# Recurrent layer with experts on one core: position network started earlier, part of VectorE's additions moved to GpSimd, all orders new

## The chip, the cores and the metric

One core of a Trainium2 chip runs the whole program. The metric is the device time of one execution in microseconds (us). The trace is one profiled execution of the same program. PE is TensorE, DVE is VectorE, ACT is ScalarE, POOL is GpSimd, SP is the engine that issues most transfers.

## The reference, cut to what matters

```python
xn = layernorm(x)                                  # x: 8 x 512 x 128, float32
u, v = split(silu(xn @ uv_w))                      # both 8 x 512 x 128
t = rpe(positions) * 0.99 ** |position|            # 3 layers of 32, then an output layer
s = (u * circular_convolution(t, v)) @ o_w         # through a transform of length 1024
rw = softmax(xn.mean(axis=1) @ Wr + br)            # one routing for each of the 8 batches
e1, e2 = top2(rw)                                  # two of 8 experts, weights by softmax
h = gelu(xn @ W1[e] + b1[e])                       # 128 -> 512, for both experts
y = sum_e weight_e * (h @ W2[e] + b2[e]) + xn
g = silu(layernorm(y) * gamma + beta)
out = x + s * g
```

`rpe` is a small network (width 32): three times `h = silu(ln(h)) @ fc`, then an output layer, on the positions 0 to 511 and their negatives.

## The kernel before

Every engine has its own instruction stream, written by hand in Python. What stands in a stream, and in which order, is set by tables (`PE_JOBS`, `ACT_JOBS`, `DVE_JOBS`, `POOL_JOBS`): each names a kind of job and, for each repetition, a place. The places are counted in tiles. A tile is one slice of 128 hidden units of one expert of one batch: 8 tiles a batch (2 experts of 4 slices), 64 in all. For tile n PE computes the hidden slice (`hidden`, bank0 or bank1; from tile 4 on in three matmuls of the types fp32r, L1119 to L1121, over an upper and a lower part of both operands), ACT applies Gelu into `h_ring` (L624), and PE multiplies by W2 (`expert_out`, L1332). Between the tiles stand the other jobs. On each engine the order is strict: a job that waits holds all that stands behind it. Place 10.03 means after the work of tile 10; places under 0 are the head.

The jobs that the text speaks of:

- `mean`, `logits`, `rank`, `shift`, `hot`, `top`, `mix`, `pick`, `sel`, `bias`: the router, for batch 0, batch 1 and batches 2 to 7 together. `rank` gives the indices with which SP fetches W1 (`w1_raw`) and W2 (`w2_s`) of the batch.
- `x_stats` (DVE), `x_root` (POOL), then normalising: `x_norm` on DVE (L772) for batches 0 and 1, `x_affine` on ACT (L490) for the rest; `x` is the transpose on PE, `x_out` the copy on ACT, `x_hi` and `x_lo` split it.
- `weights` (DVE), `rows` (PE), `matrices` (DVE), then `product`, `square`, `variance`, `eps`, `layer`, `root`, `spread`, `norm`, `tanh`, `act`: the position network.
- `w1_hi` makes the upper part of W1, `w1` on DVE the lower one (L818, 128 x 512).
- `forth` is the transform of v (six matmuls), `products`, `middle` and `join` its products with the filter on DVE, `back` the transform back (L1367), `odd` and `conv` its reading and the product with u, `mixed` the multiplication by o_w (L1391).
- `out` on DVE reads the expert sum of a batch (L808, L810), `y` transposes it (L1376), `sum` is its statistics, `root` on POOL its inverse root, `y_affine` on ACT, `norm` on DVE multiplies by gamma and adds beta (L1044, L1046), `gate` is the tanh or Silu, `weight` and `result` finish the gate and the output (L1094 multiplies, L1097 adds x).
- `lift` and `settle` do this for batch 7, with POOL giving only the root.
- `warm` is matmuls of zeros, `WARM[i]` of them in job i. `warm(0)` is also called once before the tables. Each of these matmuls leaves two records in the trace.

## Time and profile before

| | |
|---|---|
| median of 3 runs | 213.66 us (211.11 to 214.86) |
| profiled execution, time | 214.19 us |
| profiled execution, span from first to last instruction | 212.4 us |
| outside the span | 1.8 us |
| PE, DVE, ACT, POOL busy | 199.2, 171.3, 122.8, 47.0 us |
| mean granted clock of PE | 0.967 |

PE's busy time counts pipelined matmuls from issue to a modelled end, so a full PE in this table need not be at its peak rate. Work is judged by the distance from one start to the next.

### The profile page before, as it was taken

What the parts mean: (1) busy time and instruction counts of PE and PEld (TensorE: products, weight loads), DVE (VectorE), ACT (ScalarE), POOL (GpSimd) and SP (SyncE); (2) the same over time, 40 slices, a digit from 0 to 9 for tenths busy, and PEclk for the clock granted to TensorE, in tenths of its full rate; (3) what the DMA queues carried; (4) which work ended last, traced back from release to release, by engine and by line L of the source; (5) the groups of instructions that cost most, each with busy time, mean ns of one, the idle gap of its engine ahead of it and who ended that gap; (6) DMA issues with size and microseconds to landing.
All of it is one profiled execution on the core that took longest, in us unless ns stands there. A gap on an engine that the chain in (4) does not pass through costs nothing.

```text
span 212.4 us, 3224 instructions
## 1 busy us (share of the span) xinstructions
PE 199.2 (94%) x926; PEld 140.6 (66%) x926; DVE 171.3 (81%) x451; ACT 122.8 (58%) x269; POOL 47.0 (22%) x72
## 2 busy tenths in 40 slices
...
DMA packets 25173, 17.37 MB, mean 82 GB/s; under 512 B 1396, under 2 KB 22556, under 8 KB 25028
## 3 DMA queue, kind: packets, MB, share of 16 engines
...
q8 instruction: 7, 0.11, 0.2%
...
## 4 chain that ended last, share of the span: by engine, by line
PE 49%; DVE 21%; POOL 12%; issue 11%; ACT 4%; DMA 1%; DVEq 0%; POOLq 0%; ACTq 0%
PE bank L1332 13%; PE bank L1119 6%; PE bank L1120 5%; PE bank L1121 5%; PE bank L1367 4%; PE bank L1231 3%; PE bank L1172 3%; POOL rstd L678 3%; POOL layer_r L698 2%; DVE Y L991 2%; DVE ystats L745 2%; DVE prod L993 2%; POOL root L676 2%; DMA x_ring<-in_L_attn_x 1%; POOL mr L714 1%
## 5 line engine op out<-in xcount | busy, mean ns | idle before, releaser
L1332 PE MATMUL bank<-h_ring,w_s 128*128 128x512 f32 x128 | 66.4, 602 | 1.5 <-issue 0.8
L624 ACT ACTIVATE h_ring<-bank,b_sel 128x512 f32<-128x512 f32 x64 | 43.8, 688 | 37.4 <-PE bank L1121 32.9
L1119 PE MATMUL bank<-xT_hi,w_hi 128*128 128x512 f32 x60 | 41.5, 691 | 0.7 <-ACT h_ring L624 0.7
L676 POOL TENSOR_SCALAR root<-ymv 128x4 f32<-128x4 f32 x7 | 4.2, 606 | 111.6 <-DVE ymv L748 111.6
L1332 PEld LDWEIGHTS bank<-h_ring,w_s 128*128 128x128 f32 x128 | 23.3, 189 | 8.2 <-issue 2.2
L1120 PE MATMUL bank<-xT_lo,w_hi 128*128 128x512 f32 x60 | 23.7, 394 | 0.0
L1121 PE MATMUL bank<-xT_hi,w_lo 128*128 128x512 f32 x60 | 23.6, 393 | 0.0
L1119 PEld LDWEIGHTS bank<-xT_hi,w_hi 128*128 128x128 f32 x60 | 11.3, 189 | 11.5 <-issue 9.8
L1120 PEld LDWEIGHTS bank<-xT_lo,w_hi 128*128 128x128 f32 x60 | 11.4, 190 | 9.9 <-issue 9.8
L1367 PEld LDWEIGHTS bank<-inv_sb,Y 128*128 128x128 f32 x128 | 15.3, 192 | 3.3 <-issue 2.9
L1367 PE MATMUL bank<-inv_sb,Y 128*128 128x128 f32 x128 | 15.7, 276 | 0.3 <-DVE conv L1028 0.2
L991 DVE TENSOR_TENSOR Y<-bank,A_sb 128x1024 f32<-128x1024 f32 x8 | 9.7, 1216 | 5.9 <-PE bank L1121 5.9
L500 ACT ACTIVATE zb<-bank,ynmr,yrstd 128x128 f32<-128x128 f32 x28 | 10.5, 458 | 5.6 <-POOL ynmr L691 5.5
L1116 PE MATMUL bank<-h_ring 128*128 128x256 f32 x40 | 12.4, 468 | 1.4 <-DVE h_ring L961 1.4
L1121 PEld LDWEIGHTS bank<-xT_hi,w_lo 128*128 128x128 f32 x60 | 11.3, 188 | 2.6
L554 ACT ACTIVATE w_s<-w_s,cw_all 128x512 f32<-128x512 f32 x16 | 10.9, 718 | 0.3 <-DMA w_s<-in_L_ffn_W 0.3
L1116 PEld LDWEIGHTS bank<-h_ring 128*128 128x128 f32 x40 | 9.1, 239 | 2.9 <-DVE h_ring L961 1.4
L1391 PE MATMUL bank<-ow_sb,uT 128*128 128x128 f32 x64 | 8.5, 276 | 2.7 <-DVE uT L1030 2.7
L1391 PEld LDWEIGHTS bank<-ow_sb,uT 128*128 128x128 f32 x64 | 8.0, 192 | 4.3 <-DVE uT L1030 3.1
L818 DVE TENSOR_TENSOR w_lo<-w_raw,w_hi 128x512 fp32r<-128x512 f32 x15 | 10.1, 682 | 0.8 <-ACT w_hi L547 0.7
L490 ACT ACTIVATE xn<-x_ring,mr,rstd 128x128 f32<-128x128 f32 x24 | 9.9, 489 | 0.1
L993 DVE TENSOR_TENSOR prod<-bank,A_sb 128x1024 f32<-128x1024 f32 x8 | 9.7, 1214 | 0.0
...
## 6 DMA issues: line engine op xcount, KB each, us to landing
...
```

The source lines that it names most:

```text
L500: last = nc.scalar.activation(zb[:, b % 2, t], YT_PS[:, t * D:(t + 1) * D], ACT.Identity, bias=ynmr[:, t:t + 1], scale=yrstd[:, t:t + 1])
L554: nc.scalar.activation(w2_s[:, b % 2, j].rearrange("p c d -> p (c d)"), w2_s[:, b % 2, j].rearrange("p c d -> p (c d)"), ACT.Copy, scale=c ...
L624: nc.scalar.activation(h_ring[:, n % NH], H_PS[n % 2][:], ACT.Gelu, bias=b1_sel[g][:, c, j, r:r + 1]).then_inc(h_done, 1)
L991: nc.vector.tensor_tensor(y, both(v_re), filters(kc, 1 - s, 1), ALU.mult).then_inc(vre_used, 1)
L993: nc.vector.tensor_tensor(term, both(v_im), filters(kc, 1 - s, 0), ALU.mult).then_inc(vim_used, 1)
L1116: nc.tensor.matmul(H_PS[1][:, 0:PW], h_ring[:, 0, 0:P], h_ring[:, 0, 0:PW], start=True, stop=True)
L1119: nc.tensor.matmul(out_ps, w_hi, m_hi, start=start, stop=False)
L1120: nc.tensor.matmul(out_ps, w_hi, m_lo, start=False, stop=False)
L1121: return nc.tensor.matmul(out_ps, w_lo, m_hi, start=False, stop=stop)
L1332: nc.tensor.matmul(OUT_PS[:], w2_s[:, b % 2, j, c], h_ring[:, n % NH], start=(i == 0), stop=(i == HT - 1)).then_inc(w2_mm, 1)
L1367: last = nc.tensor.matmul(EO_PS[:, o:o + P], Y[:, kc, s, ri, b % GB], inv_sb[:, kc, ri], start=(kc == 0), stop=(kc == KC - 1))
L1391: last = nc.tensor.matmul(S_PS[b][:, t * P:(t + 1) * P], uT[:, b, t * P:(t + 1) * P], ow_sb[:], start=True, stop=True)
```

## The change

Four things change together. The names of lines below are those of the kernel after.

1. Position network: `position_weights` is split into `start`, which comes before the first `rank`, and `weights` (the output layer's matrix), which comes late. Its small results lie in the last two rows of `uT` and in bank3, so the first product no longer needs the second one (`rows`). Product, variance, root and spread of layer 0 now stand in the head.
2. Normalising of batches 2 to 7 goes from ACT (`x_affine`) to DVE (`x_norm`).
3. POOL takes the lower parts of W1 from batch 3 on (10 of 15), the addition of beta for batches 0 to 5, and the last addition of x for batches 0 to 6. That is 23 instructions of 128 x 512. The factor 0.5 moves into DVE's multiplication.
4. `WARM` is `[5, 1, 1, 2]` with job 0 only in the explicit call, so 9 matmuls of zeros are left of 20. All tables are new; the first tile with `u` and `v` is 12 and was 10.

```diff
-WARM = [5, 5, 3, 2]
+WARM = [5, 1, 1, 2]
...
+    ("beta", 0): [12.04, 31.01, 34.01, 50.01, 55.01, 57.02],
+    ("w1", 6): [16.01, 17.01, 22.01, 22.02, 30.01, 30.02, 37.01, 37.02, 45.01, 46.01],
+    ("add", 0): [40.01, 42.01, 44.01, 57.01, 63.01, 63.02, 63.04]})
...
-        y0, y1 = rows[:, 0], rows[:, 1]
+        y0, y1 = uT[:, B - 2], uT[:, B - 1]
...
+                        if n < B - 1:
+                            sp.wait_ge(res_done, n + 1)
+                        else:
+                            sp.wait_ge(last_done, h + 1)
...
+            def w1_lower(i):
+
+                b, j = i // TOPK, i % TOPK
+                pool.wait_ge(w1_hi_done, i)
+                nc.gpsimd.tensor_tensor(w1_lo[:, b % 2, j], w1_raw[:, j], w1_hi[:, b % 2, j],
+                                        ALU.subtract).then_inc(w1_split, 1)
+
+            def gate_beta(b):
+
+                pool.wait_ge(zm_done, b + 1)
+                nc.gpsimd.tensor_tensor(zb[:, b % 2], zb[:, b % 2], bcast(bet[:].unsqueeze(1), [P, NT, D]),
+                                        ALU.add).then_inc(zg_done, 1)
+
+            def add_x(b):
+
+                pool.wait_ge(s_read, b + 1)
+                pool.wait_ge(x_in[b], 32)
+                nc.gpsimd.tensor_tensor(x_ring[:, b], th_ring[b % NTH], x_ring[:, b], ALU.add).then_inc(res_done, 1)
...
-            def position_weights(_):
+            def position_start(_):
 
                 dve.wait_ge(rpe_in, 16 * 8)
                 dve.wait_ge(consts_in, 16)
...
                 if n == 0:
-                    pe.wait_ge(rpe_ready, 2)
+                    pe.wait_ge(rpe_ready, 1)
+                    pe.wait_ge(xmean_done, 1)
...
+                if b < PLAIN:
+                    gained.then_inc(zm_done, 1)
+                    return
+                step(gained)
+                dve.wait_ge(zg_done, b)
...
+                dve.wait_ge(s_ps, b + 1)
+                if b < B - 1:
+                    nc.vector.scalar_tensor_tensor(out=w, in0=S_PS[b][:].rearrange("p (t d) -> p t d", t=NT),
+                                                   scalar=0.5 if b < PLAIN else 1.0, in1=w, op0=ALU.mult,
+                                                   op1=ALU.mult).then_inc(s_read, 1)
+                    return
```

PE from its first instruction to its second hidden slice. `bank1<-h_ring` are the zeros, `rstd,x_ring` is `mean`, `x_ring,w1_raw` a hidden slice. Before:

```order
L1116 MATMUL bank1<-h_ring 128x256 x5
L1127 MATMUL bank5<-wr_sb,h_ring 128x8
L1116 MATMUL bank1<-h_ring 128x256 x10
L1136 MATMUL bank4<-rstd,x_ring 128x1 x4
...
L1116 MATMUL bank1<-h_ring 128x256 x3
L1259 MATMUL bank5<-c128,onehot0 8x1 x2
L1116 MATMUL bank1<-h_ring 128x256 x2
L1271 MATMUL bank5<-selT0,conv 128x2 x4
L1295 MATMUL bank4<-c128,rows 128x8
L1296 MATMUL bank4<-rows,yT 128x224
L1136 MATMUL bank2<-rstd,x_ring 128x1 x4
L1311 MATMUL bank0<-x_ring,w1_raw 128x512
```

After:

```order
L1150 MATMUL bank1<-h_ring 128x256
L1170 MATMUL bank4<-rstd,x_ring 128x1 x4
...
L1215 MATMUL bank4<-yT,uT 128x256
L1150 MATMUL bank1<-h_ring 128x256
L1296 MATMUL bank5<-c128,onehot0 8x1 x2
L1226 MATMUL bank4<-same_mean,rows 128x4 x2
L1182 MATMUL bank6<-c128,xn 128x128 x4
L1308 MATMUL bank5<-selT0,conv 128x2 x4
L1150 MATMUL bank1<-h_ring 128x256 x2
L1347 MATMUL bank0<-x_ring,w1_raw 128x512
```

One matmul of zeros instead of ten stands between the router's constants and `mean`, and the mean of batch 1 and the `rows` went behind the first hidden slice.

DVE from the expert sum of batch 7 (`yT<-bank2`) to its end. Before:

```order
L808 SCALAR_TENSOR_TENSOR yT<-bank2,b2_mix2,x_ring 128x2x128
L810 SCALAR_TENSOR_TENSOR yT<-bank2,b2_mix2,x_ring 128x2x128
L1027 TENSOR_TENSOR conv<-bank3,O_sb 128x2x128
...
L1094 TENSOR_TENSOR cs_raw<-bank6,cs_raw 128x512
L1097 SCALAR_TENSOR_TENSOR x_ring<-cs_raw,x_ring 128x512
L1056 SCALAR_TENSOR_TENSOR zb<-bank5,ymv,gam 128x128 x4
L1027 TENSOR_TENSOR conv<-bank3,O_sb 128x2x128
L1028 TENSOR_TENSOR conv<-bank3,O_sb 128x2x128
L1030 TENSOR_TENSOR uT<-uT,conv 128x512
L1066 SCALAR_TENSOR_TENSOR zb<-zb,yrstd,bet 128x128 x4
L1094 TENSOR_TENSOR th<-bank7,th 128x512
```

After:

```order
L836 SCALAR_TENSOR_TENSOR yT<-bank2,b2_mix2,x_ring 128x2x128
L1121 SCALAR_TENSOR_TENSOR cs_raw<-bank4,cs_raw 128x512
L1121 SCALAR_TENSOR_TENSOR cs_raw<-bank6,cs_raw 128x512
L771 BN_STATS ystats<-bank5 128x6 x4
L774 BN_AGGR ymv<-ystats 128x2 x4
L1121 SCALAR_TENSOR_TENSOR th<-bank7,th 128x512
L1092 SCALAR_TENSOR_TENSOR zb<-bank5,ymv,gam 128x128 x4
L1102 SCALAR_TENSOR_TENSOR zb<-zb,yrstd,bet 128x128 x4
```

Both `conv` of batches 6 and 7 went ahead of this piece, and three multiplications of batches 4, 5 and 6 without their additions stand in it.

POOL at its end in the kernel after (before, only the groups of `root`, `ynmean`, `yrstd` and `ynmr` stood here):

```order
L685 TENSOR_TENSOR yrstd<-root,minus_half 128x4
L698 TENSOR_TENSOR ynmr<-ynmean,yrstd 128x4
L752 TENSOR_TENSOR x_ring<-cs_raw,x_ring 128x512 x2
L691 TENSOR_SCALAR root<-ymv 128x4
L692 TENSOR_TENSOR yrstd<-root,minus_half 128x4
L752 TENSOR_TENSOR x_ring<-th,x_ring 128x512
```

Two additions of x come ahead of the last root, one behind it.

## Rows read from the trace of the kernel before

**Rows 1.** The page's first line.
```profile
span 212.4 us, 3224 instructions
```
**Rows 2.** Windows: busy PE, PEld, DVE, ACT, POOL; clock; DMA.
```profile
34.05:147.54 113.49, 112.44 (x538) 81.06 (x538) 93.23 (x229) 81.80 (x186) 24.16 (x35) 1.00 0.25 72
147.54:164.96 17.42, 16.77 (x65) 10.99 (x64) 15.83 (x27) 9.35 (x17) 4.02 (x4) 1.00 0.42 122
164.96:180.18 15.22, 14.96 (x53) 9.16 (x51) 15.05 (x26) 8.22 (x13) 2.33 (x4) 1.00 0.18 52
180.18:197.72 17.54, 16.41 (x80) 11.12 (x80) 15.30 (x32) 10.09 (x19) 2.05 (x4) 1.00 0.11 31
197.72:212.40 14.68, 6.93 (x58) 6.33 (x56) 11.02 (x33) 1.63 (x5) 1.27 (x2) 0.87 0.30 89
```
**Rows 3.** The timeline of the head: start, us, engine, line.
```profile
5.59 1.02 POOL L708 TENSOR_TENSOR rstd<-var_eps,minus_half 128x4 f32<-128x4 f32 x1 [4.60 <-DVE neg_mean L759]
6.16 5.14 PE L1116 MATMUL bank<-h_ring 128*128 128x256 f32 x20
11.13 0.95 PE L1136 MATMUL bank<-rstd,x_ring 128*128 128x1 f32 x8
14.16 1.52 SPq L416 DMA_DIRECT2D w_raw<-in_L_ffn_W  x2
15.88 0.21 DVE L867 COPY rows<-rows 8x128 f32<-8x128 f32 x1
16.87 0.15 DVE L876 TENSOR_SCALAR same_mean<-c 128x4 f32<-128x4 f32 x1
19.52 2.06 PE L1311 MATMUL bank<-x_ring,w_raw 128*128 128x512 f32 x2
57.15 0.15 DVE L898 SCALAR_TENSOR_TENSOR logit<-bank,br_sb 6x8 f32<-6x8 f32 x1 [0.36 <-PE bank L1251]
```
**Rows 4.** PE alone in a window: us, busy, granted clock, DMA.
```profile
18.00:24.00 6.00, 6.00 (x17) 0.50 0.53 168
```
**Rows 5.** DVE alone in a window of the head.
```profile
20.00:57.15 37.15, 28.12 (x120) 0.89 0.27 85
```
**Rows 6.** The chain: start, us. Two successive tiles, `back`, `mixed`, `y`, gamma.
```profile
106.55 0.86 PE bank L1332 x2
108.10 0.86 PE bank L1332 x2
124.14 1.78 PE bank L1367 x16
135.72 0.89 PE bank L1391 x8
136.61 0.44 PE bank L1376 x4
175.21 0.61 DVE zb L1044
```
**Rows 7.** Beta's group, and from the timeline normalising on DVE.
```profile
L1046 DVE TENSOR_TENSOR zb<-zb,bet 128x512 f32<-128x512 f32 x7 | 4.8, 692 | 0.2
7.01 1.11 DVE L772 TENSOR_SCALAR xn<-x_ring,mv,rstd 128x128 f32<-128x128 f32 x4
```
**Rows 8.** POOL in the timeline: a large operation, and small ones beside DVE.
```profile
15.12 0.45 POOL L726 TENSOR_TENSOR uw_lo<-O_sb,uw_hi 128x128 fp32r<-128x128 f32 x1
24.63 0.23 POOL L677 TENSOR_SCALAR xnmean<-mv 128x4 f32<-128x4 f32 x1
155.11 1.11 POOL L676 TENSOR_SCALAR root<-ymv 128x4 f32<-128x4 f32 x1 [13.43 <-DVE ymv L748]
154.94 1.19 DVE L1006 TENSOR_TENSOR Y<-Y,prod 128x1024 f32<-128x1024 f32 x1
```
**Rows 9.** The timeline of the tail.
```profile
208.42 0.42 DVE L1089 TENSOR_TENSOR th<-bank,th 128x256 f32<-128x256 f32 x1
209.66 0.43 DVE L1091 TENSOR_TENSOR x_ring<-th,x_ring 128x256 f32<-128x256 f32 x1
```

More of the change, by code:

```diff
@@ new lines @@
+    ("bias", 0): [-1.91, 5.03, 12.16], ("pick", 0): [-1.49, 5.51, 12.19], ("root", 0): [-1.47, 5.02, 10.02, 12.13],
+    ("sel", 0): [-1.46, 6.52, 12.23], ("rows", 0): [-1.45],
[3 rows of a table added]
+    ("forth", 0): [12.3, 15.01, 18.01, 23.52, 34.01, 39.52, 42.01, 47.52],
+    ("back", 0): [31.51, 34.02, 35.51, 37.01, 55.52, 57.01, 59.01, 60.51],
+    ("mixed", 0): [39.51, 40.51, 42.02, 45.51, 63.01, 63.02, 63.04, 63.05]}, 2)
+ACT_JOBS = by_tile({
+    ("uw", 0): [-0.99], ("means", 0): [-0.98, 2.01], ("square", 0): [-0.97, 3.02, 9.02, 14.03],
+    ("x_out", 0): [-0.96, 2.02, 2.04, 6.01, 7.01, 9.01, 12.01, 13.02], ("half", 0): [-0.95, 3.01, 14.07],
[4 rows of a table added]
+    ("filter", 0): [14.26, 14.31], ("turned", 0): [14.29, 15.03],
+    ("y_affine", 0): [14.3, 27.01, 36.01, 51.01, 57.01, 59.01, 61.01],
+    ("gate", 0): [15.01, 34.03, 36.05, 53.01, 58.02, 60.01, 62.01, 63.02], ("keep", 0): [15.02, 25.01, 41.01, 49.01],
+    ("w1", 6): [17.01, 18.01, 23.01, 23.02, 31.01, 31.02, 39.01, 39.02, 47.01, 47.02],
+    ("odd", 0): [34.01, 36.04, 38.01, 39.03, 58.01, 59.02, 61.02, 63.01]})
```

140 lines of the change are left out of this document (63 added, 77 removed), and 13 rows, old and new, of tables (ACT_JOBS, PE_JOBS).

## The prediction

> **What bounds the kernel now.** I read the windows by stage first, then the chain, then the timelines of head and tail. I cut the windows where DVE reads the expert sum of batch 4, 5, 6 and 7, at 147.54, 164.96, 180.18 and 197.72 us. The reader should see three regimes [rows 2]. Up to 34 us is the head, in which the first hidden slice starts only at 19.52 [rows 3]. From 34.05 to 147.54 us PE is busy 112.4 of 113.5 us and the chain stays on it: two tiles start 1.55 us apart [rows 6], and nothing but PE's own work counts. From 147.54 on DVE is busy 15.8 of 17.4, 15.1 of 15.2 and 15.3 of 17.5 us, and behind 197.72 it works off what is left, alone, in 14.7 us [rows 2].
>
> How much PE waits in the 50.2 us from 147.54 to 197.72 follows from prices. A tile is 1.55 us, of which `expert_out` is 0.86, so one of the three fp32r matmuls is 0.23; `forth` has six, 1.4. `back` is 1.78, `mixed` 0.89, `y` 0.45 [rows 6]. The table puts there 24 tiles, three `forth`, two `back`, one `mixed`, three `y`: 37.3 + 4.2 + 3.6 + 0.9 + 1.3 = 47.3 us. So PE waits 2.9 us for DVE, less than DVE's fullness suggests. What makes the end late is the 14.7 us behind.
>
> **The head, -3.5 us (0 to -6).** The inverse root of batch 0 is there at 6.61 us, but 20 records of zeros, ten matmuls, hold PE until 11.3 us, and `mean` starts at 11.13 [rows 3]. With one matmul there (about 0.5 us) it can start near 6.8, 4.3 us sooner. Against it stands the new `start` on DVE, ahead of `rank`: six small operations, 1.1 us by the same ones at 15.88 to 17.02 [rows 3], and a wait for eight small transfers whose landing no row shows; their issues end at 4.6. I let it cost up to 1 us beyond its own 1.1 in the likely case; part of both hides behind the mean. Then W1 is asked for near 11 instead of 14.16 [rows 3]. Between this and the first hidden slice, `rows` and the second mean (2.6 us, half of it at the low clock) have left PE. I put the first hidden slice at 15 us, for 19.52.
>
> The other end of this stage is DVE's read of the logits of batches 2 to 7, at 57.15 us [rows 3]: it comes when all eight x are transposed. In the new tables it has moved from tile 10 to tile 12, so 2 x 1.55 = 3.1 us more of PE's work lies ahead of it. From 19.52 to 57.15 are 37.6 us; 15 + 37.6 + 3.1 = 55.7. Two costs come on top. PE's clock is 0.50 from 18 to 24 us [rows 4], which cost some 3 us there; with fewer zeros in a sparse stretch I expect more of it, +1.2 us (0 to 3). And DVE now normalises six more batches, 1.11 us each [rows 7], 6.7 us: 28.1 us of work in 37.15 [rows 5] become 34.8 in about 41, still less than full, though a queue that full waits more. So the point lies at 56.9 us, 0.25 sooner, with 3.1 us more done: 3.35, and ACT, which loses the six batches, gives a little: -3.5. The low end is a DVE that fills up: 34.8 us with the waits of before (9 us) are 43.8, some 3 more, and the gain is gone.
>
> **The middle, tiles 12 to 39: 0.** PE is the bound there and its work is the same. DVE loses `w1` and beta, 0.61 us each of the chain's time (0.69 from start to end, the operations overlap) [rows 6, 7]; neither is on the path. ACT's Gelu waits for POOL's root only if POOL is late; POOL is busy 24.2 of 113.5 us [rows 2] and gets some 15 large operations, at most 18 us more.
>
> **The order of PE, +3.6 us at 197.72.** `mixed` 0 to 2 and `y` 3 moved from ahead of tile 40 to behind it: 3.1 us out of one stage and into the next, no gain. `back` 6 and 7 moved from behind the last sum to ahead of it: 3.6 us more PE work before it. The stretch of the 50.2 us now holds 37.3 + 4.2 + 7.1 + 3.6 + 1.8 = 54.0 us of PE.
>
> **PE's waits for DVE, -1.4 us (0 to -2.9; on the bad side, the rival below).** DVE's work between the sums of batches 4 and 6 is, at 0.6 us for 512 columns and 1.2 for 1024 [rows 6, 8], 33 us: `products` 5 to 7, two `middle` and two `join` of 3.6 each are 25.2, `conv` 3 is 1.3, three `result` 1.8, two `out` 1.6, two `sum` 2.6, a `norm` 0.6. PE's is 16 tiles, three `forth`, four `mixed` and two `y`: 24.8 + 4.2 + 3.6 + 0.9 = 33.5. Behind it DVE has, counted in the same way, 13.8 us against PE's 20.5. So the balance is tight for 33 us and loose for 20. Of the 2.9 us of waits I leave 1.5.
>
> What an addition costs on POOL no row shows at this size. `uw_lo`, 128 x 128, took 0.45 us, small ones 0.23 [rows 8]. Line through both: about 0.0018 us per column, 1.1 to 1.2 us at 512, an estimate; from below, 0.69 us, what DVE takes. The 23 operations are some 27 us of POOL, on top of 47. What they do to DVE is the second unknown. A root of four columns, 0.23 us alone, took 1.11 us beside DVE's L1006, and ended at 156.22 when that ended at 156.13 [rows 8]: POOL waited for DVE. The reverse can't be seen, since POOL's operations are tiny there; L1006, 1.19 us, is what 1024 columns take. I take 0, the reading of the nearest row, and leave the rest to the rival.
>
> The Trainium skill, "SBUF — State Buffer", section "Who interferes with whom", says that a DVE instruction with two SBUF inputs and a GpSimd instruction that reads SBUF share a read interface, and that the second to issue fully blocks until the first is done. The trace agrees for POOL behind DVE, by the row above; for DVE behind POOL it is open. By that rule the sum would be that of the first rival.
>
> **The tail, -3.9 us (-2.7 to -4.3).** Now it takes 14.7 us: sum, `conv` 6 and 7, lift, settle, three results, with the last DVE instruction ending at 210.09 and the last store 2.3 us later [rows 2, 9]. After, counted from the last `out`: PE does `mixed` 4 and 5, then `y` 7, done at 2.2 us, while DVE multiplies for batches 4 and 5. Statistics 2.4 to 3.7; the third multiplication to 4.3; lift to 5.35. POOL adds x of batches 4 and 5 by 4.0, then takes root and power, 1.3 us, to 5.4; settle 5.5 to 6.6; half the Silu runs beside it; the last four operations are 1.67 us (208.42 to 210.09 [rows 9]), to 8.3; store 2.3: 10.6. Batch 6's addition on POOL ends about 6.9 and its whole store may be last; I add 0.2: 10.8. `conv` has been paid before the sum, where DVE has 6 us to spare.
>
> **Sum.** On the profiled execution's 214.19 us (212.4 [rows 1] + 1.8): -3.5 + 3.6 - 1.4 - 3.9 = -5.2, so 209.0 us. That execution is 0.5 us above the median of 213.66; the three runs spread over 3.7 us, so I keep 209.0.
>
> **Rivals.**
> 1. POOL holds DVE. If each large operation on POOL stops DVE for its 1.2 us: between the sums of batches 4 and 6 stand six of them (two `w1`, three `add`, one `beta`), 7.2 us on a DVE with 0.5 us to spare; and the last `add`, beside settle, 1.2 in the tail. 209.0 + 6.7 + 1.2 = 216.9, slower than before. It decides from about half the price on: at 0.6 us each the time is 213. For it: POOL does wait for DVE. Against it: DVE's operation beside POOL's root was not longer than its like [rows 8], and where DVE has slack anyway it costs nothing. Chance 0.13 for the full price.
> 2. The head gives nothing: the eight transfers come late, or the half clock lasts, or DVE, 6.7 us heavier, sets the pace. 209.0 + 3.5 = 212.5. Chance 0.22.
> 3. It gives all: DVE's idle time in the head shrinks, waits of PE vanish. Head -6, waits -2.9: 209.0 - 2.5 - 1.5 = 205.0. Chance 0.17.
> 4. The new additions on POOL take nothing off the path, because DVE's queue was never what the tail waited for: then -1.4 and half of the tail's gain go: 212.3. DVE's fullness speaks against it. It is counted in 2.
>
> **How the numbers follow.** The forecast of 209.0 (207 to 211) has 0.48. A measurement of this kernel tells about 2%, 4.3 us: faster is below 209.4. Faster: half and a little more of the forecast, 0.29, rival 3, 0.17: 0.46, and a little from a head between: 0.48. Slower, above 217.9, is the upper part of rival 1: 0.06. Same: 0.46. The range goes from 204 to 214.5, which leaves out the far part of rival 3 and rival 1.
>
> **What the changed profile would show.** `mean` near 7 us, W1's first transfer issued near 11, the first hidden slice near 15; the logits of six rows at 57, behind twelve tiles. POOL's additions of 128 x 512 at 1.2 us. DVE's two-input operations still 0.69 us apart from POOL's; if they read 1 us and more beside POOL, rival 1 is at work. From the last `out` to the end 10.8 us. Wrong would be: the clock at 0.50 for more than 12 us in the head, PE waiting for DVE over 5 us between tiles 40 and 55, or a root on POOL late behind its additions so that ACT's Gelu waits.

## The result, and the profile after

The changed kernel takes **218.43 us** (median of 5 runs, 218.23 to 220.79) beside 213.66 us before: 1.028 times as long, 95% interval 1.021 to 1.034. I had forecast 209.0 us and a range from 204 to 214.5. It is slower, and outside the range. (Ratios in this document, and the column *kept* of the table below, leave out runs in which the clock stayed low for longer than in the others, so a ratio can differ a little from the quotient of the medians beside it.)

The top of the page of the changed kernel:
```profile
span 219.0 us, 3195 instructions
...
PE 198.5 (91%) x904; PEld 139.7 (64%) x904; DVE 171.4 (78%) x452; ACT 116.3 (53%) x247; POOL 81.0 (37%) x95
...
PEclk9856999699999999999999999999999997599995
```
POOL went from 47.0 to 81.0 us. DVE should have lost 15.7 us (ten lower parts, six betas, seven sums with x, at 0.68 to 0.69 each [rows 7]) and gained 6.7 (normalising, 1.11 each [rows 7]), which makes 162 from 171.3. It stands at 171.4. Nine microseconds of DVE were handed back by something. (This execution took 220.8 us, the slowest of the five; by the table below about 1.6 of the 2.4 us above the median are its head, and 0.9 lie between tiles 43 and 63, where e10, with the same order there, loses 8.2 us for its 9.1.)

The windows, cut again where DVE reads the logits of six batches and the expert sums of batches 4 to 7 (us, then busy PE, PEld, DVE, ACT, POOL; clock; DMA), to hold against [rows 2]:
```profile
57.55:145.24 87.69, 84.83 (x398) 61.53 (x399) 67.92 (x135) 56.75 (x121) 25.62 (x25) 1.00 0.24 67
145.24:166.56 21.32, 20.80 (x95) 14.60 (x94) 21.11 (x23) 9.68 (x16) 9.78 (x5) 1.00 0.36 111
166.56:182.25 15.69, 13.82 (x47) 7.87 (x45) 15.35 (x31) 7.87 (x15) 7.05 (x8) 1.00 0.13 36
182.25:207.13 24.88, 21.41 (x105) 16.35 (x106) 14.14 (x39) 15.19 (x28) 9.60 (x13) 0.86 0.08 22
207.13:219.00 11.87, 3.97 (x36) 3.78 (x34) 8.72 (x25) 0.83 (x2) 4.99 (x5) 0.81 0.38 110
```
In the second row DVE is busy 21.1 of 21.3 us with 23 instructions, nearly 1 us each; before it had 27 in 15.8 us. The fourth row is where the gain of the head has gone: 24.9 us for 17.5, of which some 3 are work that the new order puts there (two `back` and a `y` more, a `mixed` less), and a clock of 0.86.

Why DVE's instructions are long shows in the groups (mean ns of one behind the busy time); before, the four of DVE read 1.21 to 1.23 us:
```profile
L1050 DVE TENSOR_TENSOR Y<-Y,prod 128x1024 f32<-128x1024 f32 x4 | 7.0, 1756 | 0.0
L1049 DVE TENSOR_TENSOR Y<-Y,prod 128x1024 f32<-128x1024 f32 x4 | 6.9, 1728 | 0.1
...
L1039 DVE TENSOR_TENSOR prod<-prod,A_sb 128x1024 f32<-128x1024 f32 x4 | 6.8, 1707 | 0.1
...
L1024 DVE TENSOR_TENSOR prod<-bank,A_sb 128x1024 f32<-128x1024 f32 x8 | 9.7, 1213 | 0.0
...
L739 POOL TENSOR_TENSOR w_lo<-w_raw,w_hi 128x512 fp32r<-128x512 f32 x10 | 15.2, 1535 | 26.3 <-ACT w_hi L554 26.3
```
and, one by one, in the timeline, first at the second `join`, then at two `products`:
```profile
118.67 3.50 POOL L739 TENSOR_TENSOR w_lo<-w_raw,w_hi 128x512 fp32r<-128x512 f32 x2 [7.42 <-ACT w_hi L554]
118.74 2.28 DVE L1049 TENSOR_TENSOR Y<-Y,prod 128x1024 f32<-128x1024 f32 x1
120.94 2.30 DVE L1050 TENSOR_TENSOR Y<-Y,prod 128x1024 f32<-128x1024 f32 x1
...
92.85 1.28 POOL L739 TENSOR_TENSOR w_lo<-w_raw,w_hi 128x512 fp32r<-128x512 f32 x1 [5.07 <-ACT w_hi L554]
93.07 1.22 DVE L1024 TENSOR_TENSOR prod<-bank,A_sb 128x1024 f32<-128x1024 f32 x1
```
POOL began 0.07 us ahead of L1049, and L1049 took its own 1.23 plus 1.05 us; it ran again only when POOL's 1.28 us were over. Then POOL's second operation waited for DVE, and L1050 for that. L1024 reads one input from PSUM, and stayed at 1.22 beside the same operation. So in this trace a `tensor_tensor` with both inputs in SBUF waits for POOL, one with an input in PSUM doesn't.

The late stall, tiles 57 to 59:
```profile
177.54 0.88 DVE L771 BATCH_NORM_STATS2 ystats<-bank 128x6 f32<-128x128 f32 x4
...
178.92 1.11 POOL L683 TENSOR_SCALAR root<-ymv 128x4 f32<-128x4 f32 x1 [3.72 <-DVE ymv L774]
...
181.37 1.86 POOL L685 TENSOR_TENSOR yrstd<-root,minus_half 128x4 f32<-128x4 f32 x1
...
183.54 1.51 ACT L504 ACTIVATE zb<-bank,ynmr,yrstd 128x128 f32<-128x128 f32 x4 [2.93 <-POOL ynmr L698]
...
185.19 1.09 PE L1412 MATMUL bank<-c,yT 128*128 128x128 f32 x4 [3.76 <-ACT zb L504]
...
186.07 3.62 PE L1403 MATMUL bank<-inv_sb,Y 128*128 128x128 f32 x16
```
The statistics of batch 4's gate come late on DVE, POOL's root and power run slowly beside `join` (0.23 and 1.04 us for batches 0, 1 and 3 in this trace), so that POOL's part of the gate, from the statistics to `ynmr`, takes 4.7 us for 2.0; ScalarE waits for it, and PE waits 3.76 us for the bank before it can do `y` of batch 5. Behind the gap the clock is low, and `back` takes 3.62 us for 1.78 [rows 6]:
```profile
184.00:190.50 6.50, 5.31 (x23) 4.82 (x23) 2.90 (x12) 2.39 (x6) 3.31 (x5) 0.50 0.00 0
```
Timeline of the head and tail of the changed kernel, for [rows 3] and [rows 9]:
```profile
6.71 1.03 PE L1170 MATMUL bank<-rstd,x_ring 128*128 128x1 f32 x8
...
9.77 1.22 PE L1215 MATMUL bank<-yT,uT 4*128 4x256 f32 x2 [1.58 <-DVE uT L902]
...
11.21 1.52 SPq L417 DMA_DIRECT2D w_raw<-in_L_ffn_W  x2
...
17.74 1.91 PE L1347 MATMUL bank<-x_ring,w_raw 128*128 128x512 f32 x2
...
57.55 0.15 DVE L929 SCALAR_TENSOR_TENSOR logit<-bank,br_sb 6x8 f32<-6x8 f32 x1 [1.20 <-PE bank L1288]
...
212.77 1.26 POOL L752 TENSOR_TENSOR x_ring<-th,x_ring 128x512 f32<-128x512 f32 x1
212.90 2.07 DVE L1102 SCALAR_TENSOR_TENSOR zb<-zb,yrstd,bet 128x128 f32<-128x128 f32 x4 [0.39 <-POOL yrstd L692]
```
and the head's window, with its clock of 0.57:
```profile
8.00:20.00 12.00, 10.42 (x34) 6.76 (x34) 7.70 (x41) 1.63 (x6) 4.09 (x5) 0.57 0.73 204
```

**One measure for all kernels.** A tile is marked by the start of its third fp32r product. Between two marks PE's work is known: 1.55 a tile, 1.78 a `back`, 0.89 a `mixed`, 0.44 a `y`, 1.4 a `forth` [rows 6]. What a stretch lasts beyond that I call *lost*: PE's waits and its half clock. Tiles 15 to 43 hold 62.9 us of work before and 59.3 after (three `mixed` and two `y` fewer), tiles 43 to 63 hold 39.1 and 43.6 (e2, e3, e13, e14 as before; e8, e9, e16 with a `y` 0.4 earlier; e12 and the kernels of the early end by what their tables hold). Profiled executions, us:

| kernel | tile 15 at | lost 15-43 | lost 43-63 | last `out` to end | span | median | kept | ratio |
|---|---|---|---|---|---|---|---|---|
| before | 89.0 | 0.2 | 2.5 | 14.7 | 212.4 | 213.66 | | 1 |
| after | 86.7 | 2.9 | 9.1 | 11.9 | 219.0 | 218.43 | 218.4 | 1.028 |
| e1 POOL tiny | 84.8 | 0.1 | 4.8 | 10.6 | 208.7 | 210.65 | 207.4 | |
| e2 dummies | 86.8 | 5.2 | 5.6 | 15.3 | 219.4 | 222.10 | 222.1 | 1.035 |
| e3 offload only | 89.7 | 0.8 | 1.4 | 14.6 | 212.1 | 213.07 | 213.1 | 0.995 |
| e4 back on DVE | 85.1 | 4.2 | 9.3 | 12.5 | 219.9 | 221.31 | 221.3 | 1.032 |
| e5 W1 tiny | 85.4 | 0.8 | 7.1 | 11.9 | 213.7 | 215.58 | 215.5 | 1.009 |
| e8 early gates | 83.9 | 2.9 | 7.4 | 11.9 | 214.5 | 217.17 | 217.2 | 1.015 |
| e9 e8, W1 on DVE | 85.1 | 4.0 | 10.4 | 11.9 | 219.8 | 221.70 | 221.7 | 1.032 |
| e10 zeros in head | 83.5 | 2.9 | 8.2 | 11.9 | 215.0 | 218.16 | 217.5 | 1.018 |
| e11 placed | 85.3 | 1.0 | 5.7 | 11.9 | 212.4 | 214.62 | 214.2 | 0.999 |
| e12 late end | 85.3 | 2.9 | 8.1 | 15.7 | 219.3 | 220.98 | 221.0 | 1.031 |
| e13 placed hybrid | 85.1 | 1.4 | 1.1 | 14.6 | 207.9 | 210.08 | 209.7 | 0.979 |
| e14 hybrid | 89.0 | 2.4 | 1.5 | 14.6 | 213.1 | 213.58 | 211.7 | 0.988 |
| e15 e13, early end | 85.0 | 1.5 | 1.1 | 12.2 | 214.7 | 216.14 | 215.9 | 1.007 |
| e16 e8 and e11 | 85.5 | 1.1 | 4.1 | 11.9 | 211.1 | 213.72 | 213.2 | 0.999 |
| e17 e15 reordered | 85.2 | 1.5 | 1.1 | 12.2 | 210.5 | 212.07 | 212.1 | 0.991 |

Before's median was 213.9 to 214.3 in the later sessions. The changed kernel was timed in the first one only, so its distance to the others holds some half a microsecond of doubt. Each experiment has one trace, and what a stretch loses in it is a reading of that one.

### The profile page after: what moved, and what is told of

It is laid out like the page before. It is cut to its first block, busy times and chain, and to the rows that moved or that the text cites. A ratio compares the mean times of both kernels' runs of the same rounds, so it can differ in the third digit from the quotient of the medians.

```text
span 219.0 us, 3195 instructions
## 1 busy us (share of the span) xinstructions
PE 198.5 (91%) x904; PEld 139.7 (64%) x904; DVE 171.4 (78%) x452; ACT 116.3 (53%) x247; POOL 81.0 (37%) x95
## 4 chain that ended last, share of the span: by engine, by line
DVE 21%; issue 12%; PE 10%; POOL 7%; ACT 2%; DVEq 0%; ACTq 0%; POOLq 0%
PE bank L1403 4%; POOL yrstd L685 3%; PE bank L1368 3%; DVE prod L1039 3%; DVE Y L1022 2%; DVE prod L1024 2%; DVE ystats L771 2%; DVE Y L1037 2%; ACT zb L504 1%; DVE Y L1050 1%; POOL x_ring L752 1%; DVE prod L1048 1%; POOL root L683 1%; POOL ynmean L684 1%; DVE prod L1041 1%
## 5 line engine op out<-in xcount | busy, mean ns | idle before, releaser
L1153 PE MATMUL bank<-xT_hi,w_hi 128*128 128x512 f32 x60 | 43.4, 724 | 0.0
L739 POOL TENSOR_TENSOR w_lo<-w_raw,w_hi 128x512 fp32r<-128x512 f32 x10 | 15.2, 1535 | 26.3 <-ACT w_hi L554 26.3
L1403 PEld LDWEIGHTS bank<-inv_sb,Y 128*128 128x128 f32 x128 | 16.9, 209 | 4.9 <-issue 3.1
L1403 PE MATMUL bank<-inv_sb,Y 128*128 128x128 f32 x128 | 17.5, 295 | 2.1 <-DVE Y L1050 1.3
L1154 PEld LDWEIGHTS bank<-xT_lo,w_hi 128*128 128x128 f32 x60 | 11.5, 192 | 11.2 <-issue 11.1
L683 POOL TENSOR_SCALAR root<-ymv 128x4 f32<-128x4 f32 x7 | 3.2, 458 | 33.0 <-DVE ymv L774 33.0
L745 POOL TENSOR_TENSOR zb<-zb,bet 128x512 f32<-128x512 f32 x6 | 8.7, 1447 | 12.7 <-DVE zb L1075 12.7
L1075 DVE TENSOR_TENSOR zb<-zb,gam 128x512 f32<-128x512 f32 x7 | 4.8, 690 | 10.6 <-ACT zb L504 10.6
L1150 PE MATMUL bank<-h_ring 128*128 128x256 f32 x18 | 8.6, 639 | 1.4 <-DVE h_ring L992 1.4
L1024 DVE TENSOR_TENSOR prod<-bank,A_sb 128x1024 f32<-128x1024 f32 x8 | 9.7, 1213 | 0.0
L1412 PE MATMUL bank<-c,yT 128*128 128x128 f32 x32 | 5.3, 294 | 4.5 <-ACT zb L504 4.5
L726 POOL TENSOR_TENSOR ex<-e_base,ex 1x8 f32<-1x8 f32 (+1 forms) x3 | 4.9, 1627 | 11.7 <-DVE ex L937 11.7
```

Source lines behind the costliest of these rows:

```text
L739: nc.gpsimd.tensor_tensor(w1_lo[:, b % 2, j], w1_raw[:, j], w1_hi[:, b % 2, j], ALU.subtract).then_inc(w1_split, 1)
L745: nc.gpsimd.tensor_tensor(zb[:, b % 2], zb[:, b % 2], bcast(bet[:].unsqueeze(1), [P, NT, D]), ALU.add).then_inc(zg_done, 1)
L1024: nc.vector.tensor_tensor(term, both(v_im), filters(kc, 1 - s, 0), ALU.mult).then_inc(vim_used, 1)
L1153: nc.tensor.matmul(out_ps, w_hi, m_hi, start=start, stop=False)
L1154: nc.tensor.matmul(out_ps, w_hi, m_lo, start=False, stop=False)
L1403: last = nc.tensor.matmul(EO_PS[:, o:o + P], Y[:, kc, s, ri, b % GB], inv_sb[:, kc, ri], start=(kc == 0), stop=(kc == KC - 1))
```

## The experiments

**e1, e2, e3, e4: whose cost is it, POOL's or the order's?** e1 is the changed kernel with the 23 whole-tile operations on POOL cut to four columns:
```
-  nc.gpsimd.tensor_tensor(w1_lo[:, b % 2, j], w1_raw[:, j], w1_hi[:, b % 2, j],
+  nc.gpsimd.tensor_tensor(w1_lo[:, b % 2, j, 0:4], w1_raw[:, j, 0:4], w1_hi[:, b % 2, j, 0:4],
   (the same for beta and for the sum with x)
```


> The kernel after, with GpSimd's 23 operations of 128 x 512 cut to 4 columns each (the work that they leave out, most of the lower parts of W1 from batch 3 on, of beta and of the last sum with x, is done by nobody). All waits and orders stay. Theory A, GpSimd's large operations hold VectorE and VectorE's hold GpSimd: the time falls by 6 us or more, to 212 or below, and VectorE's 1024-column operations of 2.2 us in the trace are 1.2 us again. Theory B, the new order is itself too tight (three gate chains in tiles 55 to 62, the transpose of y put ahead of the read of its bank): 216 to 218, and TensorE still stands still for 3 us or more near the sum of batch 6.

Measured 210.65 us (its four runs: 207.39, 210.50, 210.80 and 211.35), 7.8 below the changed kernel. L1049 and L1050 are back (groups), and the wait at `y` of batch 5 is shorter but there (timeline):
```profile
L1049 DVE TENSOR_TENSOR Y<-Y,prod 128x1024 f32<-128x1024 f32 x4 | 4.9, 1226 | 0.1
L1050 DVE TENSOR_TENSOR Y<-Y,prod 128x1024 f32<-128x1024 f32 x4 | 4.9, 1219 | 0.0
```
```profile
177.12 0.94 PE L1412 MATMUL bank<-c,yT 128*128 128x128 f32 x4 [2.80 <-ACT zb L504]
```
By the table the price of POOL's large operations is 2.8 us up to tile 43, 4.3 up to tile 63 (3.4 against e10's trace) and 1.3 in the tail. What is left of the miss, 4.8 lost between tiles 43 and 63 where before lost 2.5, is not theirs. Nor are all holds gone. The 2.80 us of wait come from POOL's small operations for batch 4's gate, each held in its turn by a piece of `join`:
```profile
170.68 1.19 DVE L1048 TENSOR_TENSOR prod<-prod 128x1024 f32<-128x1024 f32 x1
170.85 1.12 POOL L683 TENSOR_SCALAR root<-ymv 128x4 f32<-128x4 f32 x1 [3.83 <-DVE ymv L774]
171.90 1.23 DVE L1049 TENSOR_TENSOR Y<-Y,prod 128x1024 f32<-128x1024 f32 x1
172.04 1.17 POOL L684 TENSOR_SCALAR ynmean<-ymv 128x4 f32<-128x4 f32 x1
173.05 1.22 DVE L1050 TENSOR_TENSOR Y<-Y,prod 128x1024 f32<-128x1024 f32 x1
173.30 1.86 POOL L685 TENSOR_TENSOR yrstd<-root,minus_half 128x4 f32<-128x4 f32 x1
```
From the statistics to `ynmr` this takes 4.7 us, for 2.0 for batches 0, 1 and 3 of the same trace. By these rows 2.7 of the 2.80 us of wait are this hold, and the low clock behind the wait makes up most of the rest of the 4.8. No run moved the gate off the `join`, so this is read from the rows and not tried.

e2 is the kernel before with 23 useless additions of 128 x 512 on POOL, and DVE keeps all its work:
```
+  def unused():
+      nc.gpsimd.tensor_tensor(rows[:, 0] (unused here), gam, bet, ALU.add)
+  ("beta", 0): [10.04, 33.02, ...], ("w1", 6): [16.01, ...], ("add", 0): [34.02, ...]
```


> The kernel before, with nothing taken off VectorE, and 23 additional additions of 128 x 512 on GpSimd, released at the places at which the change has its own (behind the upper part of W1, the read of y, the multiplication of the result). Theory A: it costs 3 to 8 us, mostly behind 147 us, where VectorE is full: 217 to 221, with single VectorE operations of two SBUF inputs longer by about 1 us. Theory B: within 1 us of the kernel before, since nobody waits for the additions.

Measured 222.10 us: 7.8 us for 23 operations on which nobody waits, a little above Theory A's range, and not mostly behind 147 us: up to tile 43 the loss grew by 5.0 us, from there to tile 63 by 3.1. DVE's busy time rises from 171.3 to 183.4, 0.53 us for each. The operations with SBUF inputs alone grew, also 512-column ones, those with PSUM did not (timeline, then groups):
```profile
107.25 1.78 DVE L843 TENSOR_TENSOR w_lo<-w_raw,w_hi 128x512 fp32r<-128x512 f32 x1
```
```profile
L1044 DVE TENSOR_TENSOR Y<-Y,prod 128x1024 f32<-128x1024 f32 x4 | 7.0, 1759 | 0.0
...
L1018 DVE TENSOR_TENSOR prod<-bank,A_sb 128x1024 f32<-128x1024 f32 x8 | 9.7, 1214 | 0.0
```

e3 is the kernel before with only the work moved (the three functions on POOL, DVE's `w1` from batch 3 on, beta and the sum with x taken out), its order kept:
```
-  ("w1", 1): [-0.81, 3.05, 7.05, 10.21, 10.29, 13.02, 17.01, 23.01, 23.03, ...],      (DVE)
+  ("w1", 1): [-0.81, 3.05, 7.05, 10.21, 10.29],                                       (DVE)
+  ("w1", 6): [16.01, 17.01, 23.01, 23.02, 31.01, 31.02, ...], beta, add               (POOL)
```


> The kernel before, its own order on TensorE, ScalarE and VectorE, with only the third part of the change: W1's lower parts from batch 3 on, beta for batches 0 to 5 and the last sum for batches 0 to 6 on GpSimd. Theory A: what VectorE gains (0.6 us for each) it loses again in holds of up to 1 us; 212 to 217. Theory B: the relief counts in full in the stages that VectorE bounds: 208 to 211.

Measured 213.07 us, 0.995 (0.991 to 0.998), as Theory A had it. DVE's busy time fell by 7.4 us, not by 15.7: half of the relief goes back in holds, and the rest is worth 1.2 us.

e4 is the changed kernel with all three kinds back on DVE:
```
-  ("beta", 0): [12.04, ...], ("w1", 6): [16.01, ...], ("add", 0): [40.01, ...]        (POOL)
+  ("w1", 1): [..., 15.05, 18.02, 23.005, 23.015, 31.011, 31.012, 38.01, 39.011, 47.03, 47.04]   (DVE)
```


> The kernel after, its new order and head, with the three kinds of work given back to VectorE at nearly the same places. Theory A: VectorE's load rises by 14 us but no hold is left; 216 to 221, near the kernel after. Theory B: the tight order gets tighter by the whole relief: 223 or more.

Measured 221.31 us, 2.9 above the changed kernel and just above Theory A's range. So POOL's operations cost the changed kernel 7.8 us as they fall, and yet it is slower still with the same work on DVE. In it DVE is short of time: between tiles 40 and 55 it is busy 35.0 of 35.4 us. That 0.69 us more on such a DVE is worse than a hold that only sometimes lands on the path is how I read it.

**e5: which of them.** The changed kernel with only the ten W1 operations cut to four columns.

> The changed kernel with POOL's ten operations for W1's lower part cut to four columns (the rest of that lower part is left out); beta and the sum with x stay whole on POOL. Cutting all 23 gave 210.65 us for 218.4. Theory A, POOL's whole-tile operations stretch DVE's SBUF-only ones one for one, and W1's ten are those that fall beside DVE's join and middle operations: about 213.5 us, DVE's L1049 and L1050 back at 1.23 us mean in most pairs. Theory B, the price lies in the sum with x and in beta, at the end where DVE is the bound: at most 1 us off, 217.5 or more.

Measured 215.58 us, 2.9 below: halfway between the two (213.5 and 217.5). Of the 2.8 us lost up to tile 43, 2.1 are W1's, at the second `join`; of the 4.3 behind, 2.0. The sum with x and beta hold the rest: L1049 still had a mean of 1.46 us, L1039 of 1.71.

**e8, e9: the packed gates.** e8 moves two gates:
```
-  ("y", 0): [12.28, 23.51, 26.01, 47.51, 50.01, 55.51, 57.02, 63.03]
+  ("y", 0): [12.28, 23.51, 26.01, 39.53, 47.51, 55.51, 57.02, 63.03]
   ("sum": 47.02, 53.01 -> 41.01, 49.01; root, y_affine, norm, beta, gate likewise)
```


> The changed kernel with the gates of batches 3 and 4 earlier: y of batch 3 behind tile 39 and of batch 4 behind tile 47 (for 47 and 50), their sums, roots, normalisings, gammas, betas and tanh moved with them; nothing else. Theory O (order): the 3.8 us for which PE waits at y of batch 5, and the half clock behind it, come from three gates packed into tiles 50 to 59; with two of them gone the wait goes and the clock stays at 1.00: tile 59 starts 4 to 6 us sooner, 213 to 214.5 us in all. Theory P (POOL alone): DVE is merely late by what POOL took from it, and an earlier gate only moves the wait to the back transforms: within 1 us of 218.4.

Measured 217.17 us, 1.3 below, a little outside Theory P's range. The gap at tile 59 shrank (10.3 us from tile 58 to 59 became 3.8), but from tile 55 to 58 the same kernel now needs 8.7 us where the changed one needed 4.7. Theory O fell: the wait moved, as Theory P had it, though not only by what POOL took. Batch 4's statistics stood in DVE's queue for 7.6 us (162.3 to 169.9), and POOL's part of the gate again took 4.3 us for 2.0. ScalarE waited 3.03 us for it, with a Gelu behind it for which PE waited 2.16.

e9 is e8 with W1's lower parts on DVE again.

> The run before with W1's lower parts back on DVE from batch 3 on (one addition each in DVE's order at the places that the kernel of before gives them), beta and the sum with x still on POOL. Theory A says an operation on POOL costs DVE 1.2 us where it falls beside one of DVE's with SBUF inputs alone, and gives it 0.6 to 0.7: for W1, ten of them, a gain of 1 to 4 us against the run before, 210 to 213 us. Theory B, the moved operations take nothing net: equal to the run before within 1 us.

Measured 221.70 us, 4.5 above e8; both theories missed, the first in sign too. On a DVE that is short of time ten operations of 0.68 us cost more than their holds did on POOL.

**e10: the head's clock.**
```
-WARM = [5, 1, 1, 2]        ("warm", 1): [-1.99, -1.95, -1.9]
+WARM = [5, 1, 5, 1, 2]     ("warm", 1): [-1.99, -1.965, -1.95, -1.9]
```


> The changed kernel with five more products of zeros between the router's first logits and the position network's first product, where PE idles for 1.6 us; nothing else. If the clock of 0.50 from 9.8 to 19.6 us comes from that gap and from the sparse work behind it, the gap's filling keeps it at 1.00 for a part of these 10 us: the first hidden slice at 15.5 to 16.5 us for 17.74, and 1 to 2 us off the whole, 216.5 to 217.5 us. If the sparse work alone decides, the clock falls all the same and the time is within 0.5 us of 218.4.

The clock did what was expected, and more: in the window 8 to 20 us it is 0.95 for 0.57 (0.50 to 0.72 in the other twelve traces with this head), and the first hidden slice starts at 14.73:
```profile
7.96 2.43 PE L1150 MATMUL bank<-h_ring 128*128 128x256 f32 x10
...
14.73 1.02 PE L1347 MATMUL bank<-x_ring,w_raw 128*128 128x512 f32 x2
```
```profile
8.00:20.00 12.00, 11.12 (x56) 7.58 (x55) 9.91 (x55) 2.08 (x6) 4.95 (x8) 0.95 0.71 205
```
(A shorter piece at 0.50 comes later, from 18.8 to 22.2 us.)
Tile 15 is at 83.5, the earliest of all, 3.2 us ahead of the changed kernel's trace but 1.7 ahead of the median (85.2) of the other kernels with this head. The whole is 218.16 us in the median of four runs that spread from 216.74 to 220.86 (217.5 without the highest, beside 218.4): no difference that I can tell. The clock's cause is shown, a gain of time isn't.

**e11, e12: placing POOL's operations; the end.** e11 is the changed kernel with the same 23 operations, four groups of which wait for something (six operations):
```
-  ("w1", 6): [..., 30.01, 30.02, ...]           +  ("w1", 6): [..., 33.02, 33.03, ...]     (POOL)
+  if b == 5: pool.wait_ge(conv_done, 1)         # W1's pair, not beside the second join
+  if b == 7: pool.wait_ge(Y_done, 6)            # W1's pair, not beside the third join
+  if b in (1, 2): pool.wait_ge(Y_done, 6)       # sum with x, not beside middle and join
```


> The changed kernel with the same 23 whole-tile operations on POOL, four pairs of them placed: W1's pair for batch 5 waits for the first convolution, that for batch 7 and the sums with x of batches 1 and 2 for the third join, so that they run beside DVE's operations with an input in PSUM or in its idle time. In the trace of the changed kernel those with an input in PSUM kept 1.22 us beside POOL, and those with SBUF inputs alone went from 1.23 to 2.2. Theory A with this limit: DVE's L1049 and L1050 fall from 1.73 and 1.76 us mean to 1.4 or less, 3 to 4 us off, 214.5 to 215.5 us. Rival: POOL takes a fixed share wherever it runs, and the time stays within 0.7 us of 218.4.

Measured 214.62 us, 3.8 below the changed kernel, as Theory A had it. They now run beside operations that read PSUM, and neither waits; `join` is whole again:
```profile
156.79 1.22 DVE L1028 TENSOR_TENSOR Y<-bank,A_sb 128x1024 f32<-128x1024 f32 x1
156.89 1.27 POOL L758 TENSOR_TENSOR x_ring<-th,x_ring 128x512 f32<-128x512 f32 x1 [10.67 <-DVE Y L1056]
```
```profile
L1055 DVE TENSOR_TENSOR Y<-Y,prod 128x1024 f32<-128x1024 f32 x4 | 4.9, 1225 | 0.1
L1056 DVE TENSOR_TENSOR Y<-Y,prod 128x1024 f32<-128x1024 f32 x4 | 4.9, 1218 | 0.0
```
(L1055 and L1056 are L1049 and L1050 of the changed kernel.) Same work on the same engines, only its neighbours are others: this is what shows the mechanism, and not only POOL's total. What it leaves is batch 4's gate: POOL's part of it takes 4.7 us here too, and PE waits 3.72 us at `y` of batch 5.

e12 puts the end back as before the change:
```
-  ("back", 0): [..., 59.01, 60.51]    ("mixed", 0): [..., 63.01, 63.02, 63.04, 63.05]
+  ("back", 0): [..., 63.01, 63.04]    ("mixed", 0): [..., 60.01, 63.02, 63.05, 63.06]
```


> The changed kernel with the back transforms and convolutions of batches 6 and 7 behind the last expert output again, and mixed of batch 4 ahead of it, as before the change. My prediction booked +3.6 us for moving them ahead and -3.9 us for the tail. If both terms were right: within 1 us of 218.4, the last stage 3 to 4 us longer and that before it 3 to 4 us shorter. If DVE is the bound on both sides, the convolutions cost the same at either place: also the same total, but the stage before gets shorter by less than 2 us. If the wait at y of batch 5 needs them there: 1 to 3 us faster.

Measured 220.98 us, 2.6 above: outside all three. The tail grew by 3.8 us, while the way from tile 15 to the last `out` became only 2.1 shorter. In the new order the early end pays. (Against e10's trace, with the changed kernel's order there, that way is 1.3 shorter.)

**e13, e14: the old order behind tile 30.** e14 keeps the changed kernel's tables up to tile 30 and takes those of before from there on, with POOL's work; e13 adds three waits on POOL in the manner of e11 (W1's pair for batch 5: `Y_done` 4; beta of batch 3: `Y_done` 6; beta of batch 4: `middle_done` 4; the tanh of 3 and 4 at 50.005 and 57.01 for 47.01 and 55.01).

> The changed kernel's program with its tables up to tile 30 (the new head, the router and the transposes two tiles later) and the tables of before from tile 30 on (for gates, back transforms, mixed, convolutions and results; W1, beta and the sum with x on POOL as in the run that offloads in the old order). Theory O: the new head is worth 3 to 4 us and the new order behind tile 30 costs all that was lost beyond POOL's price: 213.1 of that run less 3.5 = 209.5 us (208 to 211). Rival: the head's gain melts away behind it as PE then waits for DVE: 212 to 213 us.

Median 213.58 us (211.01 to 215.16), ratio 0.988 (0.982 to 0.994). The profiled execution had a bad head, at half clock from 8 to 31 us, tile 15 at 89.0:
```profile
8.00:20.00 12.00, 10.72 (x41) 6.96 (x38) 7.82 (x42) 1.87 (x7) 4.27 (x5) 0.50 0.73 202
```
Behind the head it loses 3.9 us up to tile 63, where the changed kernel loses 12.0. Neither theory's number was met by the median (nor by the 211.7 of the column *kept*); with the head of the others, 85.2, this execution would stand near 211.

> The hybrid of the next run with three groups of POOL's operations placed: W1's pair for batch 5 waits for the second join, beta of batch 3 for the third join, beta of batch 4 for the last middle product; the tanh of batches 3 and 4 stand later on ScalarE for that. Each keeps a 1.0 us hold off a DVE operation with SBUF inputs alone, four in all; what lies on the path is some half: 1 to 3 us below the hybrid, 207 to 209 us. Rival: DVE has slack enough in this order, so 0 to 0.5 us.

Measured **210.08 us**, 0.979 (0.973 to 0.985): faster than both kernels, though the interval reaches to less than 2% below the kernel before. From tile 15 to the end it needs 122.8 us, e14 124.1: 1.3 us for the placing, in the expected range (2.0 by the column *kept*). The rest of the difference between the two spans is the head, 3.9 us by tile 15.

**e15, e17: the early end in that order.** e15 is e13 with `back` 5 to 7 at 59.01, 60.02, 61.51 and the convolutions with them, ahead of the last `out`.

> The placed hybrid (210.08 us) with the back transforms and convolutions of batches 5, 6 and 7 ahead of the last expert output, as the change has them, and nothing else of its order. In the changed kernel the reverse edit cost 2.6 us. Theory O2, the early end is sound by itself and the cost of the new order lies in its packed gates and late mixed: 207 to 209 us, the last DVE output to the end below 12 us for 14.6. Rival: DVE in this order is as full in the last tiles as in the changed kernel, PE waits for it there and what the tail gives is lost ahead of it: 210 to 212 us.

Measured 216.14 us, 6 above e13, worse than the rival. The tail did shrink to 12.2 us, but the way from tile 63 to the last `out` took 11.2 us for 3.7. The rows show why; each is held by the one above:
```profile
190.99 1.04 POOL L719 TENSOR_TENSOR yrstd<-root,minus_half 128x4 f32<-128x4 f32 x1
...
192.34 1.50 ACT L538 ACTIVATE zb<-bank,ynmr,yrstd 128x128 f32<-128x128 f32 x4 [4.14 <-POOL ynmr L732]
...
193.87 0.69 DVE L1115 TENSOR_TENSOR zb<-zb,gam 128x512 f32<-128x512 f32 x1 [2.77 <-ACT zb L538]
...
195.21 0.42 DVE L1098 TENSOR_TENSOR conv<-bank,O_sb 128x256 f32<-128x256 f32 x1
...
196.10 3.75 PE L1443 MATMUL bank<-inv_sb,Y 128*128 128x128 f32 x16 [3.53 <-DVE conv L1099]
```
The convolution needs nothing of the gate; it only stands behind it in DVE's queue. e17 takes it out of there:
```
 ACT  odd(6), odd(7): 62.02, 63.005 -> 61.95, 62.9     y_affine(6): 62.01 -> 63.005
 DVE  conv(6): 61.02 -> 61.0                           norm(6): 61.01 -> 62.5
```


> The run before with the early end (216.14 us) and three places swapped: ScalarE copies the odd parts of batches 6 and 7 ahead of normalising batch 6's gate, and VectorE does both convolutions ahead of that gate's gamma and beta. In its trace the convolution of batch 6 stood in VectorE's queue behind gamma, which waited 2.8 us for ScalarE and that 4.1 us for POOL's power; PE waited 3.5 us for it and ran at half clock behind. Theory Q, what an early end costs is this queueing behind the gate's chain: PE's wait at the last back transform goes, 208 to 211 us. Rival, the early end costs by DVE's load: above 214 us.

Measured 212.07 us: 4.1 below e15, so queueing was two thirds of it (Theory Q, a little outside its range), and 2.0 above e13. Tile 63 comes 1.9 us later for one `back` of 1.78, the last `out` another 3.2 later, and the tail gives 2.5.

**e16** is e8 and e11 together.

> The changed kernel with both edits tried apart: the gates of batches 3 and 4 earlier (that gave 1.3 us) and the four pairs of POOL's operations placed (that gave 3.8). Theory C, with the holds gone DVE has time for earlier gates, and PE's wait at y of batch 5 goes without another in its place: more than the sum, 210 to 212 us. Rival: PE's waits in the new order are DVE's work itself, wherever the gates stand: 213 to 214.5 us, about the sum or less.

Measured 213.72 us, 4.7 below the changed kernel, where the two edits alone gave 1.3 and 3.8: the rival's range. Even so, 4.1 us are lost between tiles 43 and 63. Batch 4's gate is held here too: POOL's part takes 4.3 us, ScalarE waits 2.62 us for it, and PE 1.74 us for the Gelu behind.

## Why the prediction was wrong

By its own terms, on the profiled executions (+6.6 us of span, for a sum of -5.2):

- **The head, -3.5: about right in size, in part by luck.** At tile 15, with equal work behind both, the changed kernel is 2.3 us ahead. Of thirteen kernels with exactly its head twelve stand at 83.9 to 86.7 (the median of all is 85.2) and one at 89.0 (e14); three with the old one stand at 86.8, 89.0 and 89.7. That is -2 to -4, with the clock's scatter of the head in it. The step inside it failed: first slice at 15, found at 17.74, because the clock was 0.50 there for longer than I had let it cost (+1.2). With zeros in the gap (e10) it started at 14.73. From its first slice to tile 15 the changed kernel took 69.0 us, the kernel before 69.5, where I had booked 1.2 more for the clock; so one miss made up for a part of the other. `mean` at 6.71, W1 at 11.21 and the logits at 57.55 came as said.
- **The order of PE, +3.6: 2.7.** I had left out that `mixed` of batch 4 moves the other way, 0.9 us. (The stretch of 50.2 us before the change holds two `mixed`, not one: 48.2 us of work, and so PE's waits there were 2.0, not 2.9, by my own prices.)
- **The middle, 0: failed, +2.7.** "Neither is on the path" was true of what DVE loses. What POOL adds came onto it: two W1 operations beside the second `join` made L1049 and L1050 2.1 us longer, and the first `back` waited for DVE. With POOL tiny the loss is 0.1.
- **PE's waits for DVE, -1.4: failed, and this is the step that decided.** Between tiles 43 and 63 the loss rose from 2.5 to 9.1 us, +6.6. I had written "I take 0, the reading of the nearest row" for what POOL does to DVE. That row [rows 8] had DVE's operation ahead by 0.17 us, and so could show only POOL waiting; it said nothing of the other order, which I did note and then booked as evidence. The hold is 1.05 us where a large operation starts just ahead. 4.3 of the 6.6 us are this (e1; 3.4 of 5.7 with e10's trace). My rival 1 had the mechanism, nearly its price (1.2) and, within 1.5 us, the sum (216.9), with a chance of 0.13.
- **The other 2.3 us are the new order's.** I counted 33 us of DVE against 33.5 of PE and called it tight, then took 1.4 off the waits all the same. Without the large holds (e1, e11, e16) 4 to 6 us remain lost there, wherever two of the gates stand. The old order behind tile 30, with the same work, loses 1.1 to 1.5 (e13, e14), so it isn't DVE's work as such. Two things show in the rows. The new order fills DVE between tiles 40 and 55; first e1, then e13, in the order of [rows 2]:
```profile
137.28:169.26 31.98, 31.98 (x134) 21.80 (x133) 31.05 (x44) 17.23 (x31) 5.63 (x10) 1.00 0.32 91
142.08:171.76 29.68, 29.40 (x111) 19.12 (x110) 24.11 (x43) 17.95 (x32) 13.72 (x14) 1.00 0.35 99
```
  PE loses only 0.1 us in that stretch of e1, but batch 4's statistics wait 3.6 us in DVE's queue. And they stand just ahead of `join`, which then holds POOL's small operations by 2.7 us, with PE's `y` of batch 5 waiting at the end. I had the row for this, a root of 1.11 us beside DVE, and put no price on it: I priced what POOL does to DVE, at 0, and not what DVE does to the gate's chain on POOL.
- **The tail, -3.9: -2.8.** 1.3 us are POOL again: the last sum with x began 0.13 us ahead of settle, and made it 2.07 us for 1.13. In e1 the tail is 10.6, near the 10.8 forecast. I had POOL's addition there at the right time, and priced only POOL's own lateness.

The terms sum to -2.3 + 2.7 + 2.7 + 6.6 - 0.3 (tile 63 to the last `out`) - 2.8 = 6.6. With POOL's operations cut to four columns the kernel takes 210.65 us, 1.7 above my 209.0. So the price of POOL, taken as 0, is most of the miss. That the rest came so near is in part luck: in e1's trace PE's waits are still 2.3 us up where I had 1.4 off, and a better head (-4.2), a cheaper order (+2.7) and the tail (-4.1) make up for it.

Of my signs of being wrong, two did not come: from tile 40 to 55 only 2.5 us are lost, the 6.5 us of the late stall lie behind, and the clock was 0.50 for some 10 us of the head (9.6 to 19.9), not for 12. The third nearly did: POOL's root was late, but beside DVE's `join` and not behind its own additions. What gave rival 1 away is the line before them, DVE's two-input operations at over 1 us.

The Trainium skill, "SBUF — State Buffer", section "Who interferes with whom", gives this rule and its limit: a DVE instruction with two SBUF inputs contends with a GpSimd one that reads SBUF, and one with at most one SBUF input doesn't, outside the faster modes. By that the trace agrees in both halves: 1.23 became 2.28 us for L1049, and L1024 stayed at 1.22. I cited the first half beside my 0, and let one row stand against it.

What stays open: how the 4 us that e16 still loses divide between DVE's full queue and the hold on batch 4's gate. No run moved that gate off its neighbours with two SBUF inputs, and the gates of batches 5 and 6 and the late `mixed` weren't tried apart. For the early end I can say that it costs 2.0 us in the order of e13 and saves 2.6 in the changed one; the two don't add up to one price.
